# A decoder block in one program: the first attention's loops exchanged, and the recurrence spread over it

## The reference

```
x = x + attention(layernorm(x))      # 16 heads of 128, causal, biases
x = x + wkv(layernorm(x), ctx)       # per channel, along the 128 tokens of a row
x = x + moe(layernorm(x))            # 16 experts of 176, top 4, and a shared one of 704
...
# wkv, step by step: q = max(p, u+k); y = (e^(p-q) a + e^(u+k-q) v) / (e^(p-q) b + e^(u+k-q));
#                    p, a, b carried on with the decay w
```

## Time and profile before

| | |
|---|---|
| time, median of 3 runs | 2100.88 us (2099.61 to 2102.44) |
| the profiled execution: its time | 2105.15 us |
| its span, first to last instruction | 2103.4 us |
| granted clock of TensorE, mean | 0.951 |
| busy: TensorE, VectorE, ScalarE, POOL | 1869.0, 1299.0, 915.9, 621.3 us |
| first attention, to the last output added | 605.70 us |
| experts, first to last unit (L1293) | 617.73 to 1236.10 us |

### The profile page before, as it was taken

The page is one execution under the profiler, slowest core; times in us unless marked ns, Lnnn a source line. Parts: engine busy times, 40 slices in busy tenths (PEclk is TensorE's granted clock), DMA queues, the critical chain, the costliest instruction groups (busy, mean ns, idle before and its releaser), DMA issues.

```text
span 2103.4 us, 26552 instructions
## 1 busy us (share of the span) xinstructions
PE 1869.0 (89%) x9570; PEld 1493.6 (71%) x9570; DVE 1299.0 (62%) x2653; ACT 915.9 (44%) x2481; POOL 621.3 (30%) x536
## 2 busy tenths in 40 slices
PE   5999999998867788789999988999779999999866
PEld 4888888887655565567776766777558888787634
DVE  6455454557876786776444445666545677656768
ACT  3444444444433333433233225656334555555546
POOL 2002002000035554456666745443132121211100
PEclk9999999999978899999999998999899999999989
DMA  3001001000040000020000010000100110000001
GB/s 139 1 1 46 1 1 46 11 1 6 1 163 6 5 6 1 0 91 0 1 1 1 0 66 1 1 1 1 40 22 25 35 37 27 21 1 1 0 1 41
DMA packets 12883, 44.57 MB, mean 21 GB/s; under 512 B 1744, under 2 KB 2512, under 8 KB 11856
## 3 DMA queue, kind: packets, MB, share of 16 engines
q1 hardware_dynamic: 12752, 42.87, 5.7%
HBM read 40.77 MB, written 2.10 MB: 20 GB/s over the span
## 4 chain that ended last, share of the span: by engine, by line
PE 38%; DVE 15%; ACT 6%; issue 5%; POOL 2%; DMA 1%; DVEq 0%; ACTq 0%; POOLq 0%
PE bank L445 6%; PE bank L447 6%; PE bank L446 6%; PE bank L867 4%; PE bank L709 2%; PE bank L728 2%; ACT cross_attention_heads L1916 2%; PE bank L841 2%; PE bank L858 2%; PE bank L830 1%; DVE cross_attention_heads L1474 1%; DVE experts L1290 1%; DVE experts L1293 1%; PE bank L717 1%; DVE cross_attention_heads L1485 1%
## 5 line engine op out<-in xcount | busy, mean ns | idle before, releaser
L1783 ACT CAST experts_split<-experts 128x512 fp32r<-128x512 f32 x112 | 69.6, 622 | 296.9 <-DVE experts L1293 296.9
L445 PE MATMUL bank<-x_channel_major,experts_split 128*128 128x512 f32 x448 | 185.1, 413 | 6.5 <-POOL experts_split L2051 5.9
L2058 POOL TENSOR_TENSOR experts_split<-experts,experts_split 128x512 fp32r<-128x512 f32 x112 | 149.1, 1331 | 138.2 <-ACT experts_split L1783 138.2
L1290 DVE TENSOR_TENSOR experts<-experts,bank 128x512 f32<-128x512 f32 x112 | 76.7, 685 | 177.8 <-ACT experts L1779 148.6
L446 PE MATMUL bank<-x_channel_major,experts_split 128*128 128x512 f32 x448 | 182.2, 407 | 0.0
L447 PE MATMUL bank<-x_channel_major,experts_split 128*128 128x512 f32 x448 | 181.8, 406 | 0.0
L2154 POOL TENSOR_TENSOR cross_attention_heads<-cross_attention_heads 128x512 f32<-128x512 f32 x64 | 73.4, 1147 | 329.3 <-ACT cross_attention_heads L1904 329.3
L579 PE MATMUL bank<-self_attention 128*128 128x256 f32 x512 | 128.3, 395 | 20.8 <-DVE self_attention L1222 20.8
L867 PE MATMUL bank<-cross_attention,cross_attention_heads 128*128 128x256 f32 x512 | 131.5, 402 | 13.1 <-DVE cross_attention_heads L1490 8.7
L579 PEld LDWEIGHTS bank<-self_attention 128*128 128x128 f32 x512 | 99.8, 197 | 39.9 <-issue 24.0
L1916 ACT ACTIVATE cross_attention_heads<-cross_attention_heads,small 128x128 f32<-128x128 f32 x256 | 99.5, 390 | 52.8 <-DVE small L1478 52.5
(11 more groups left out here) (299 smaller groups left out, 5076.1 us busy)
## 6 DMA issues: line engine op xcount, KB each, us to landing
qkv_weights_raw<-in_wqkv SPq DMA_DIRECT2D x12, 512.0 KB, 5.0
experts<-in_moe SPq DMA_DIRECT2D x3, 1536.0 KB, 13.5
bitnet_weights<-in_bitgu SPq DMA_DIRECT2D x8, 416.0 KB, 3.4
experts_far<-in_moe SPq DMA_DIRECT2D x2, 1536.0 KB, 10.6
residual<-in_x SPq DMA_DIRECT2D x4, 512.0 KB, 9.2
self_attention<-in_wo SPq DMA_DIRECT2D x4, 512.0 KB, 6.4
wkv<-in_ctxT SPq DMA_DIRECT2D x8, 256.0 KB, 2.8
context<-in_ctxT SPq DMA_DIRECT2D x4, 512.0 KB, 7.8
```

Of the source, the lines that this page charges most:

```text
L445: T.matmul(out_ap, w_hi, x_hi, start=first, stop=False)
L1290: V.tensor_tensor(e_hid[u], e_gate[u], bank[4 + 2 * u][:, :], ALU.mult).then_inc(e_gated, 1)
L2058: G.tensor_tensor(e_split[v][1], e_hid[n % 2], e_split[v][0].bitcast(F32), ALU.subtract).then_inc(e_h_lo, 1)
```

## The change

- The attention's positions run over the token groups outermost: g = p // 4, hg = p % 4. So every head group's weights are loaded and split four times, 16 positions in all, 15 of them (45 thirds) by POOL.
- There is one set of split weights, divided into thirds. A third is split anew as soon as the last fill that reads it is done (fill_done) and its raw third is there. The raw buffer holds two thirds.
- V is kept in six rows in place of two positions of four; the masked scores are turned into probabilities in place.
- The recurrence and the routing of group g start at step 16 (g + 1) + 1, beside the attention of group g + 1, for g = 0, 1, 2; those of group 3 run in the experts. WKV_UNITS is 26. POOL makes the products for g < 3.
- The recurrence's constants are set at step 8, and the context values of six chunks are loaded during the attention.

The diff, cut to its core:

```diff
-WKV_UNITS = 46
+THIRD = KT * HG * DH
+NV = 6
+WKV_UNITS = 26
...
+        wr = columns(scope, "qkv_weights_split", 3 * 2 * THIRD, F32R)
+        wqkv = [[wr.take(THIRD).rearrange("p (k c) -> p k c", k=KT) for part in range(2)] for m in range(3)]
+        raw_a = [ar.take(THIRD) for _ in range(2)]
-        v_a = [ar.take(GB * HG * DH).rearrange("p (b c) -> p b c", b=GB) for _ in range(2)]
+        v_a = [ar.take(HG * DH) for _ in range(NV)]
...
             def fill(p, i):                                   # TensorE
-                hg, g = divmod(p, NG)
-                if hg == 0:
+                g, f, m = p // NHG, 12 * p + i, i // HG
+                hi, lo = wqkv[m]
+                if p == 0:
                     pe.wait_ge(w_first, m + 1)
                 else:
-                    pe.wait_ge(w_split, 3 * (hg - 1) + m + 1)
+                    pe.wait_ge(w_split, 3 * (p - 1) + m + 1)
...
-                if n == LAST + 5:                             # TensorE, VectorE, ScalarE and POOL
-                    side.add(wkv_group(0), routing(0))
-                elif n == LAST + 9:
-                    side.add(wkv_group(1))
+                if n % 16 == 1 and n > 16:
+                    side.add(wkv_group(n // 16 - 1), routing(n // 16 - 1))
...
-            side.add(routing(1), wkv_group(2), routing(2), wkv_group(3))
+            side.add(wkv_group(NG - 1), routing(NG - 1))
...
                 if i == WKV_UNITS:
                     side.finish()
-                    side.add(routing(3))
...
             def scores(n):                                    # VectorE
-                dve.wait_ge(a_exp, n - 1)
+                dve.wait_ge(a_turned, n - 1)
...
-            def split_wqkv(hg):                               # POOL
-                s = hg % 2
-                for m in range(3):
-                    pool.wait_ge(got_wqkv[m], 16 * (hg + 1))
-                    pool.wait_ge(fill_done, 48 * (hg - 1))
+            def split_wqkv(p, m):
+                t = 3 * p + m
+                pool.wait_ge(got_wqkv[t % 2], 16 * (t // 2 + 1))
+                pool.wait_ge(fill_done, 12 * (p - 1) + HG * (m + 1))
+                G.tensor_copy(wqkv[m][0], third(t)).then_inc(pool.own, pool.tick())
+                pool.settle()
+                G.tensor_tensor(wqkv[m][1], third(t), wqkv[m][0].bitcast(F32), ALU.subtract).then_inc(w_split, 1)
...
-                if n in (16, 32):
-                    split_wqkv(n // 16 + 1)
+                side.step(2)
+                p, b = divmod(n, GB)
+                if b == 0 and 1 <= p < NHG * NG - 1:
+                    split_wqkv(p + 1, 2)
+                elif b >= 2 and p + 2 < NHG * NG:
+                    split_wqkv(p + 2, b - 2)
+                side.step(4)
...
+            def fetch_third(t):                               # SyncE
+                p, m = divmod(t, 3)
+                if 2 <= t < 5:
+                    sp.wait_ge(w_first, t - 1)
+                elif t >= 5:
+                    sp.wait_ge(w_split, t - 4)
+                D_(raw_a[t % 2], io["wqkv0"][:, p % NHG, m * THIRD:(m + 1) * THIRD]).then_inc(got_wqkv[t % 2], 16)
...
+            for p in range(1, NHG * NG):
+                for m in range(3):
+                    fetch_third(3 * p + m)
+                fetch_output(p)                               # waits for a_output and v_out of GB * (p - 1)
+                if p in (8, 12):
+                    fetch_value(p // 2 - 2)
+                    fetch_value(p // 2 - 1)
...
-            for c in range(3, NG * KT):                       # behind the experts' weights
-                fetch_value(c)
+            fetch_value(6)
+            fetch_value(7)
```

More of the change, by code:

```diff
@@ L222, in build @@
         kT_a = [ar.take(HG * GT).rearrange("p (h t) -> p h t", h=HG) for _ in range(2)]
-        v_a = [ar.take(GB * HG * DH).rearrange("p (b c) -> p b c", b=GB) for _ in range(2)]
-        Sm_a, Pm_a, PT_a, ZT_a = ([four(ar.take(512)) for _ in range(2)] for _ in range(4))
+        v_a = [ar.take(HG * DH) for _ in range(NV)]
+        P_a, PT_a, ZT_a = ([four(ar.take(512)) for _ in range(2)] for _ in range(3))
         bv_a = [ar.take(HG * DH) for _ in range(2)]
@@ L360, in build @@
         got_ident, got_identb, got_vec = semaphore("got_ident"), semaphore("got_identb"), semaphore("got_vec")
-        got_wqkv = [semaphore(f"got_wqkv{m}") for m in range(3)]
+        got_wqkv = [semaphore(f"got_wqkv{s}") for s in range(2)]
         got_wo_a = [semaphore(f"got_wo_a{s}") for s in range(2)]
@@ L437, in bit_piece, with third @@
             return i % 2, at, n, src
+        def third(t):
+            return raw_a[t % 2].rearrange("p (k c) -> p k c", k=KT)
         def tensor_program(pe):
@@ L1249, in vector_program @@
                 more = p + 1 < NHG * NG and n < NSTEP
-                if n == LAST:
+                if n == 8:
                     wkv_open()
-                if n == LAST + 5:
-                    side.add(wkv_group(0), routing(0))
-                elif n == LAST + 9:
-                    side.add(wkv_group(1))
+                if n % 16 == 1 and n > 16:
+                    side.add(wkv_group(n // 16 - 1), routing(n // 16 - 1))
                 if n < NSTEP:
@@ L2215, in sync_program @@
             D_(vec[:, :], io["vec"]).then_inc(got_vec, 16)
-            fetch_wqkv(0)
+            fetch_third(0)
+            fetch_third(1)
             D_(causal, io["causal"]).then_inc(got_causal, 16)
-            for g in range(1, NG):
+            D_(X[:, GB:2 * GB, :], io["x"][:, GB:2 * GB, :]).then_inc(got_x[1], 16)
+            fetch_third(2)
+            fetch_output(0)
+            for g in range(2, NG):
                 D_(X[:, g * GB:(g + 1) * GB, :], io["x"][:, g * GB:(g + 1) * GB, :]).then_inc(got_x[g], 16)
```

122 lines of the change are left out of this document (47 added, 75 removed).

## The result

The changed kernel takes **2117.49 us** (median of 4 runs, 2113.55 to 2123.97) where the one before, on the same chip, takes 2100.24 (4 runs, 2098.77 to 2102.44): a ratio of 1.0084, 95% interval 1.0057 to 1.0111. It is slower, by 17 us or 0.8%. The profiled execution took 2117.21 us, its span is 2115.3; against the span of before that is 11.9 us more.

The account below looks back on a forecast made before the run. TensorE bounds undisturbed attention, VectorE's order bounds it beside side work. Terms 53.8 + 20 - 16 - 60.5 + 2.5 sum to -0.2 us, so 2101 us against a median of 2100.88; range 2079 to 2129.

Parts of the forecast that it names:

- the forecast case itself: Whole kernel: the summed terms give no change, 2101 us, own range 2088 to 2115; chance 0.48.
- the windows: Attention beside side work of groups 0 to 2: side steps add 53.8 us, POOL's splits beside VectorE add 20.
- the end of attention: Steps 60 to 64 lose their 30 side steps and become bare steps of 6.3 us: -16 us.
- the experts: Expert units: 59 side steps in place of 156; 42 us of loss stay, 60.5 go.
- the start: Before the first output: third weight third and output bias load later, +2.5 us, ends -2 and +6.
- nothing: Extra loads are covered, and opening the recurrence at step 8 instead of 48 is the same work: no cost.
- signs of being wrong: Wrong if TensorE waits for POOL's split, VectorE for a value in unit 3, or steps outside the windows lengthen.
- The covers hold: Side-work windows: splits cost TensorE nothing there either, -20 us, 2081; chance 0.27.
- The shared access decides: Side-work windows: each split delays VectorE 2.8 us and all reaches TensorE, 58 us in place of 20, 2139; chance 0.14.
- Weights late: Attention positions with side work: POOL's splits come late and TensorE waits for weights, +25 us, 2126; chance 0.07.
- the side work does not leave the experts cheaply: Experts: loss hangs on full POOL and VectorE, not side steps, so only 40 us go, 2121; chance 0.04.
- The likeliest mechanism: Attention and experts: beside side work VectorE's order bounds and TensorE pays in gaps and lower clock; forecast chance 0.48.

Follow-up runs that it names:

- e1: The changed kernel with POOL's weight splits cut to two columns from position 1 on (output not the reference's); 2078.83 us, ratio 0.9895 to the kernel before.
- e2: The changed kernel with POOL's splits cut to two columns only in the ten steps of each side-work window (output not the reference's); 2089.24 us, one run.
- e5: The changed kernel with bias load earlier, recurrence opened at step 9, and four side steps per attention step, all behind the copies; 2069.65 us, ratio 0.9875.
- e9: The changed kernel with bias load earlier, recurrence opened at step 9, and three side steps per attention step, slots 2 to 4; 2060.42 us, ratio 0.9814.
- e6: The changed kernel with the output bias loaded ahead of the third weight third and the recurrence opened at step 9, not 8; 2099.54 us, ratio 0.9997.
- e7: The changed kernel with side work put back where the kernel before had it, POOL still making group 2's products; 2119.54 us, ratio 1.0107.

## Why the prediction was 16.5 us too low

It said no change, 2101, and gave slower by 0.2% 0.42; the measurement is 2117.5, inside the range of 2079 to 2129 but above the 2088 to 2115 of the forecast case itself. Step by step, in the terms of its sum:

1 and 2, **the windows**: 53.8 + 20 = 73.8 forecast, 73.7 measured. Both halves stand by themselves: e1 and e2 take 21.7 and 20.0 out of the windows, near the 20 of the splits, and the rest is the side work. Seven steps inside took 84.88 (outputs 31 to 38), for about 84. The agreement to a tenth is luck; the groups had 30.7, 33.5 and 32.0. The estimate of 0.96 us a split was measured at 1.0. It was a product of two guesses, 1.6 us on VectorE (between 0.6, where the row gives 1.35/2 or nearer 0.7, and 2.8) and a share of 0.6 that reaches TensorE; no run measures the two apart, so that their product came out is partly luck.

By the Trainium skill (SBUF — State Buffer, Terms) the loser of the shared access blocks fully for the whole instruction, and the prediction read this as 3.6 us for each of 20.7 splits, 75 us, where e1 and e2 show 20 to 22. What fails is that reading, and not the rule: in the rows above the sum at 260.40 ends at 263.15, 0.56 us behind the end of the subtraction beside it (259.90 + 2.69), where alone it takes 0.69. An instruction of VectorE that begins inside a split waits for the rest of the split and no more, and TensorE pays only when it then has to wait itself. The runs agree with the Trainium skill (GPSIMD Engine Reference, Key points) as to which instructions suffer.

3, **the end of attention**: -16 forecast, -16.0 measured; the last five outputs take 30.5, for 30.7. The parts were less exact than the sum: the bare steps take 6.0 and not 6.3, and the first of the five takes 7.39.

4, **the experts**: -60.5 forecast, -54.6 measured. The step that failed is "59/60 of that, 42, stay and -60.5 go". It took all of the 102.5 for side work. But 4.6 of excess stay between units 20 and 61 of the changed kernel, where it has no side work any more: two of its units take 6.64 us instead of 4.42, one of them from 33 to 34 above. All the kernels without side work there have the same two (e5 and e9 with 6.63), so before will have paid them too, inside its excess, though its rows can't show it apart. The other 1.5 is in the first 20 units, 43.5 for 42.

5, **the start**: +2.5 forecast with ends -2 and +6, measured +10.3. The step that failed counted the bias load as coming "about 6 us" late and set against that the 2.03 us of before "as it ran under the splits, which are now later". They are later, and so is the normalisation: the one delay pushed it into the other. Two lateness terms in one chain can't be netted without asking where the second lands.

6, **"nothing"**: the loads were covered: of TensorE's 3.3 us of waits for projections in the page's row 2.9 are for the first group's weights. The opening was not: "the same work on VectorE beside the same steps" overlooked that step 8 has a split of POOL beside it and step 48 of before had none. +3.6, of which e6 shows 3.5 to be that coincidence. One of the prediction's own signs of being wrong shows here: two steps outside the windows lengthened. With units 61 on (-1.7) and the way to unit 0 (-0.5) the sum comes to +14.8, the last unit of the ledger; the medians differ by 17.3.

**The rivals.** *The covers hold* (2081) is out: e1 and e2. *The shared access decides* (2139) too: 20, not 58. *Weights late* (2126) is out by the page's rows above. That *the side work does not leave the experts cheaply* (2121) came near in its number, but not in its cause: 54.6 of 60.5 went. The likeliest mechanism was right in size. The errors were in the two terms that I had priced at nothing or nearly so, 7.8 and 3.6 us, and in the experts, 5.9. The first two are also what e7 shows: what made this kernel slower came with the exchange of the loops, 13.5 us at the start and the opening and 17.0 at the last unit, and not with the side work's move, which is nearly even. With both mended (e6) the kernel is as fast as before, 0.9997.

## What to carry to other kernels

Before costing an edit at nothing, look up which heavy instruction of another engine runs in the step that it moves to: two of the three terms that failed here were small pieces of VectorE work that came to lie beside a POOL split, once because a load was one place further back in a queue. When side work shares an engine with the main chain, its place in the step counts for more than its amount: put it behind the instructions that TensorE waits for, on every engine that has one, and only then spread it. To output 58 the three groups' side work costs 96 us with six slots, 82 thinned to four evenly, 62 with four behind the copies and 35 with three. The last has its price elsewhere: the last five outputs take 6 us more than in the changed kernel, and some 20 of the 165 side steps are left for the experts, whose excess grows by 12.

## What the runs showed of the hardware

The cost of POOL beside VectorE, as TensorE feels it, changed with the schedule: the splits cost 20.0 to 21.7 us over 20 in the windows with long waits, 35.4 in e5's arrangement and 21.2 over 30 in e9's. One part of it is that longer windows have more splits beside them (about 25 by their starts). The rest of e5's cost may be that in the changed kernel late instructions partly ran into waits that were there anyway; no run separates these two.

What POOL does to VectorE is a wait for an end, and not a slower rate. Instructions with both inputs in SBUF went from 0.69 to 2.75 us (L1076 at 260.40), and a 128x516 addition of a constant from 0.49 to 2.15 (L1036 at 126.34). How long each takes goes by where in the split it begins, but each ends at its own fixed distance behind POOL's instruction: 0.55 us for 128x512 with two inputs (260.40 here, 192.02 in the trace of before, 237.60 in e5), 0.28 for the 128x516 at 126.34, 1.09 for a scan (that at 256.67 ends at 258.99, POOL's product beside it at 257.90). Reciprocals and reads from PSUM kept their time: 1.75 us for a reciprocal at 233.95 in e9 that has a split beside nearly all of it, 0.66 for L1203 at 265.05. POOL waits in the same way when VectorE is first: its cast at 257.84 took 1.98 us where 1.04 is usual and ended 0.83 behind the scan beside it, and its subtraction at 264.12 took 3.14 for 2.38. And TensorE's granted clock was lower where it waited: 0.94 in the stretch 362 to 525 of the changed kernel, 1.00 in the same stretch of e9, though VectorE had more to do in it.
